# Attention and expert layer on one core: the first loads split over two DMA queues, with fewer products of ones

## Chip, cores, metric

The kernel runs on one core of a Trainium2 chip. The metric is the device time of one execution in microseconds (us); lower is better. "Rows" of a DMA are the contiguous pieces that it moves, one or more for each of the 128 partitions.

## What is computed

Two layers on 4096 tokens (2 batches of 2048) of width 512, all in float32: cross attention with relu in place of softmax against 128 context rows for each batch, and a mixture of eight experts of which each token uses two.

```python
h  = layernorm(x)
qp = relu(h @ Wq + bq); kp = relu(ctx @ Wk + bk); vp = relu(ctx @ Wv + bv)
s  = relu(qp @ kp.T) / sqrt(512) + mask
x  = x + relu(s @ vp)
h  = layernorm(x)
topv, topi = top_k(h @ gate_w, 2);  w = softmax(topv)
x  = x + sum over the two chosen experts e of  w_e * ((silu(h @ Wu[e]) * (h @ Wv[e])) @ Wo[e])
```

## The kernel before, in words

Everything is written out by hand, engine by engine, with semaphores: each engine (TensorE `pe`, ScalarE `act`, VectorE `dve`, GpSimd `pool`, and the sync engine `sp`, which issues DMAs) runs its own list in order. The order of work is thus the order of the calls in each list.

The attention part goes over the tokens in 16 blocks of 256 (`body(Step(n))` on each engine): normalise x (`norm1`), turn it (`turn_x`), project it to queries (`queries`), form scores against the keys, attend. The products of blocks are made as three products of halves of the numbers (a high part HI, written by ScalarE's `copy`, and the rest LO, written by VectorE's `sub`). Then 71 tiles of 128 tokens, sorted by expert, go through the expert layer (`tile_body`). GpSimd scatters rows of the second norm to DRAM and stores the results with indirect DMAs.

Before the first block stands a prologue, and the change lies in it:

- **sp** (lines 440 to 449) issues the loads: the context `ctxT` (128 partitions, rows of 1 KB, 512 KB in all), the key weights `wk_raw` in four quarters of 256 KB (rows of 2 KB), block 0 of x into `xin` (512 KB, rows of 2 KB), the key bias `bk_sb`, the value weights `wv_raw` (1 MB), the query weights `wq_raw` in two halves of 512 KB, and the value bias. Then follow small constants, block 1 of x (line 469), the mask and the first expert's weights.
- **pe** (lines 1755 to 1763) first multiplies a tile of ones by itself (line 1757, result unused), then runs `keys()` (16 products of 128x256 for four chunks c of the context's width, line 1557), `values(0)` (4 products of 128x512, line 1565), `turn_x` of block 0 (line 1543), `values(1)`, and the first block's `queries` (lines 1547 to 1549).
- **act** runs `norm1(Step(0), 1)` (line 802: normalises one of the two tiles of x of block 0), then `relu_key` for the four key banks (line 788), then the high parts of the query weights (line 782, tile `wq`), of the turned x (`qT`), of the keys (`kpT`), and of the values.
- **dve** waits for block 0 of x, takes its statistics (`moments1`, lines 1158 to 1166), waits for GpSimd's reciprocal root (line 662), writes `nmr` (line 1170) and the other tile of the normalised x (line 1311), then the low parts of the query weights, the value sum of batch 0 (line 1000, tile `zb`), the low parts of `qT` and `kpT` (all line 979), the value sum of batch 1, and goes on to the statistics of block 1.

On ScalarE the norm of block 0 stands ahead of `relu_key` in the list:

```python
            norm1(Step(0), 1)
            act.wait_ge(w_loaded["bk"], 16)
            for m in (2, 3, 0, 1):
                relu_key(m)
            for c in range(DC):
                act.wait_ge(w_loaded[f"wq{c // 2}"], 16)
                copy(wq[:, HI, c, :], wq_raw[:, c, :], wq_hi)
```

Of the kernel before, what the change touches and what calls it, by code (L numbers as in the profile page):

```python
# [14 lines left out]
P = 128  # L15
LOG_P = 7
D = 512
DC = D // P
# [60 lines left out]
def ge(eng, sem, value):  # L79

    if value <= 0:
        return
    eng.wait_ge(sem, value)
# [22 lines left out]
def moe_block(nc, x, ctx_in, mask, kq, kk, kv, bq, bk, bv, gate_w, Wu, Wv, Wo, out):  # L106
    ctx = ExitStack()
    with ctx:
# [6 lines left out]
        def sem(name):  # L115
            return ctx.enter_context(nc.semaphore(name))
# [38 lines left out]
        zT, ctxT = zT_ctxT[:, 0, :, :], zT_ctxT[:, 1, :, :]  # L155
# [8 lines left out]
        def raw(e):  # L164

            return wuv[:, e, :, :].rearrange("p h n -> p (h n)").bitcast(F32)

        wk_raw = raw(E - 1).rearrange("p (c n) -> p c n", c=DC)
        wv_raw = raw(E - 2).rearrange("p (c n) -> p c n", c=DC)
# [109 lines left out]
        conv_ready = sem("conv_ready")  # L279
        ones_ready = sem("ones_ready")  # L280
        ones_used = sem("ones_used")
        w_loaded = {k: sem(f"load_{k}") for k in ("ctx", "wk0", "wk1", "wk2", "wk3", "wq0", "wq1", "wv", "bk", "small", "bv")}
        wq_hi = sem("wq_hi")
        wq_ready = sem("wq_ready")
        k_done = sem("k_done")
# [89 lines left out]
        w_v = {k: w.rearrange("a b (c p) n -> p (a b c) n", p=P) for k, w in (("q", kq), ("k", kk), ("v", kv))}  # L375
# [33 lines left out]
        def x_of(b):  # L409

            return xbuf[b.x]
# [25 lines left out]

        @block.sync
        def _(sp):
            sp.dma_start(ctxT[:, :, :], ctx_in.rearrange("(c p) k -> p c k", p=P)).then_inc(w_loaded["ctx"], 16)  # L440
            for c in range(DC):
                sp.dma_start(wk_raw[:, c, :], w_v["k"][:, c, :]).then_inc(w_loaded[f"wk{c}"], 16)
            sp.dma_start(xin[:, 0, :, :], x_blk[0]).then_inc(x_loaded[0], 16)
            sp.dma_start(bk_sb[:, :], bk).then_inc(w_loaded["bk"], 16)
            sp.dma_start(wv_raw, w_v["v"]).then_inc(w_loaded["wv"], 16)
            for h in range(2):
                sp.dma_start(wq_raw[:, 2 * h:2 * h + 2, :], w_v["q"][:, 2 * h:2 * h + 2, :]).then_inc(w_loaded[f"wq{h}"], 16)
            sp.dma_start(bv_rows, bv.rearrange("(a n) -> a n", a=1).broadcast_to([P, D])).then_inc(w_loaded["bv"], 16)
# [67 lines left out]
            def load_z(t):  # L516
                for g, (first, _) in enumerate(PARTS):
                    if t == first:
                        part_ready(g)
                if t == 0:  # L520
                    sp.wait_ge(xn_turned, 2 * NB)
                if t == 2:
                    sp.wait_ge(q_done, DC * NB)
                if t == 9:
                    sp.wait_ge(s_done, NB)
                if t == 15:
                    sp.wait_ge(o_done, 2 * NB)
                if t == 18:
                    sp.wait_ge(stage_lo, 3 * E)
                q = t % RING  # L530
                if t >= RING:
                    sp.wait_ge(res_stored[q], landed(t - RING))
                    if is_held(t - RING):
                        sp.wait_ge(aside_stored, 16 * (t - RING - FULL + 1))
                sp.dma_start(zg_of(t), z_dram[bass.ds(row_of(t), P)]).then_inc(z_loaded[q], 16)
# [244 lines left out]
        def _(act):  # L780
# [18 lines left out]
            def norm1(b, t):  # L799

                ge(act, nmr1_ready, b.n + 1)
                nc.scalar.activation(xn[:, t, 0:D], x_of(b)[:, t, :], ACT.Identity, bias=nmr1[:, t:t + 1],
                                     scale=rstd1[:, t:t + 1]).then_inc((xn0_ready, xn1_ready)[t], 1)
# [30 lines left out]
            def expert_high(b):  # L834
                if b.p == 0:
                    act.wait_ge(stageA_loaded, 32 * (b.j + 1))
                else:
                    act.wait_ge(stageB_loaded, 48 * (b.j + 1))
                for dst, src in expert_parts(b):
                    copy(dst(HI), src, stage_hi)  # L840
# [27 lines left out]
            def body(b):  # L868
# [47 lines left out]
                if nxt.real:  # L916
                    expert_high(nxt)

            norm1(Step(0), 1)
            act.wait_ge(w_loaded["bk"], 16)  # L920
            for m in (2, 3, 0, 1):
# [619 lines left out]
        def _(pe):  # L1541
# [8 lines left out]

            def keys():

                pe.wait_ge(w_loaded["ctx"], 16)
                for c in range(DC):
                    pe.wait_ge(w_loaded[f"wk{c}"], 16)
                    for m in range(DC):
                        ins = pe.matmul(ps_key[m][:, 0:BT], wk_raw[:, c, m * P:(m + 1) * P], ctxT[:, c, :],
                                        start=(c == 0), stop=(c == DC - 1))
                ins.then_inc(k_done, 1)

            def values(g):

                pe.wait_ge(w_loaded["wv"], 16)
                for c in range(DC):
                    ins = pe.matmul(ps_out[g][:, :], ctxT[:, c, g * KEYS:(g + 1) * KEYS], wv_raw[:, c, :],
                                    start=(c == 0), stop=(c == DC - 1))
                ins.then_inc(v_done, 1)
# [141 lines left out]
            def expert_of(t):  # L1709
                if t not in expert:  # L1710
                    for g, (first, _) in enumerate(PARTS):
                        if t == first:
                            pe.wait_ge(sched_ready, 2 * (g + 1))
                    expert[t] = pe.value_load(sched_exp[0:1, t:t + 1], min_val=0, max_val=E - 1)
                return expert[t]
# [37 lines left out]
                    expert_of(0)  # L1753

            pe.wait_ge(ones_ready, 1)
            for n in (D, D, P):
                ins = pe.matmul(psT[0][:, 0:n], xn[:, 0, 0:P], xn[:, 0, 0:n], start=True, stop=True)
            ins.then_inc(ones_used, 1)
            keys()
            values(0)  # L1760
            pe.wait_ge(const_ready, CONSTS)
            turn_x(Step(0))
            values(1)
            for n in range(NB):
                body(Step(n))
# [63 lines left out]
```

## Time and profile before

| | |
|---|---|
| time, median of 3 runs | 416.95 us (416.0 to 418.0) |
| time of the profiled execution | 416.64 us |
| its span in the profile | 414.9 us |
| TensorE busy | 398.1 us (96%) |
| VectorE / ScalarE / GpSimd busy | 331.6 / 277.8 / 210.3 us |
| moved by DMA | 87.66 MB, mean 211 GB/s |

Times in the profile count from the start of the span. A busy share is an average over stages with different limits; the chain of waits, which is followed back from the last instruction, says what set the time in a given stretch. Ends of matmuls are modelled, so the starts are the safer numbers. In float32 one matmul of the program stands as two records in the profile. "Landing" is the moment at which a DMA's semaphore is complete.

### The profile page before, as it was taken

The page shows a single profiled execution, that of the slowest core. Times are in us where ns is not written, and L with a number is a line of the kernel's source. Part 1 is how long each engine was busy: PE and PEld are TensorE (multiplying, and loading weights), DVE is VectorE, ACT ScalarE, POOL GpSimd, SP SyncE. Part 2 cuts the span into 40 slices and gives each one's busy share as a digit, 9 for nine tenths or more (in the row PEclk, how much of TensorE's full clock was granted, in tenths as well). Part 3 has the DMA queues.
Part 4 walks back from the last instruction along what each step waited for, and adds up shares of the span by engine and source line. Part 5 has one row for each costly group of instructions (what it writes and reads, how often), then busy time and mean ns, then how long its engine had stood idle before and what let it go on. Part 6 is the DMA issues. An engine that isn't in the chain of part 4 may idle for free.

```text
span 414.9 us, 10266 instructions
## 1 busy us (share of the span) xinstructions
PE 398.1 (96%) x3031; PEld 356.1 (86%) x3031; DVE 331.6 (80%) x1108; ACT 277.8 (67%) x596; POOL 210.3 (51%) x227
## 2 busy tenths in 40 slices
PE   8999999999999999999999999999999999999980
PEld 5588899999999999998878988898999999999960
DVE  2678899999999999998787888877887666666760
ACT  1777888888998888888767666666676444444420
POOL 3011125666555565655435545453333567778882
PEclk9999999999999999999999999999999999999995
DMA  7813424677666766443695359779976799997794
GB/s 286 284 65 102 137 92 167 243 256 245 247 233 228 256 212 225 172 164 136 186 315 204 132 187 372 293 267 315 306 237 183 209 242 291 287 248 118 109 108 90
DMA packets 49557, 87.66 MB, mean 211 GB/s; under 512 B 7648, under 2 KB 18400, under 8 KB 49376
## 3 DMA queue, kind: packets, MB, share of 16 engines
q1 hardware_dynamic: 35600, 52.37, 38.9%
q0 software_dynamic: 13904, 34.62, 29.4%
q8 instruction: 28, 0.46, 0.5%
q14 instruction: 25, 0.20, 0.1%
HBM read 44.77 MB, written 48.29 MB: 224 GB/s over the span
## 4 chain that ended last, share of the span: by engine, by line
PE 69%; DVE 15%; issue 5%; ACT 4%; POOL 4%; POOLq 0%; DVEq 0%; ACTq 0%
PE psQ L1547 12%; PE psQ L1548 11%; PE psQ L1549 11%; PE psT L1543 11%; DVE qT L979 2%; PE psO L1547 2%; DVE st L1158 2%; POOL out_dram L686 2%; PE psO L1548 2%; PE psO L1549 2%; PE psZ L1547 2%; PE psZ L1549 2%; PE psZ L1548 2%; PE psQ L1543 2%; PE psS L1547 2%
## 5 line engine op out<-in xcount | busy, mean ns | idle before, releaser
L979 DVE TENSOR_TENSOR qT<-psT,qT 128x512 fp32r<-128x512 f32 x103 | 69.5, 689 | 27.2 <-ACT qT L782 26.8
L629 POOL DMA_INDIRECT z_dram<-zb x64 | 69.3, 1083 | 39.1 <-DVE zb L1267 21.4
L1547 PE MATMUL psQ<-wuv,qT 128*128 x284 | 86.3, 304 | 0.8 <-DVE qT L979 0.4
L1548 PE MATMUL psQ<-wuv,qT 128*128 x284 | 80.2, 283 | 0.0
L1549 PE MATMUL psQ<-wuv,qT 128*128 x284 | 80.1, 282 | 0.0
L1547 PE MATMUL psQ<-qT,wq 128*128 128x256 f32 x256 | 75.2, 294 | 1.5 <-DVE qT L979 1.4
L1549 PE MATMUL psQ<-qT,wq 128*128 128x256 f32 x256 | 72.4, 283 | 0.0
L1548 PE MATMUL psQ<-qT,wq 128*128 128x256 f32 x256 | 72.3, 283 | 0.0
L782 ACT ACTIVATE qT<-psT 128x512 fp32r<-128x512 f32 x103 | 59.4, 593 | 12.1 <-PE psT L1543 12.1
L1547 PEld LDWEIGHTS psQ<-wuv,qT 128*128 128x128 f32 x284 | 53.7, 189 | 5.5 <-issue 1.4
L850 ACT ACTIVATE gate_work<-psQ 128x128 f32<-128x128 f32 x71 | 19.7, 277 | 54.5 <-PE psQ L1549 54.4
L1548 PEld LDWEIGHTS psQ<-wuv,qT 128*128 128x128 f32 x284 | 54.0, 190 | 0.0
L1549 PEld LDWEIGHTS psQ<-wuv,qT 128*128 128x128 f32 x284 | 54.0, 190 | 0.0
L1547 PEld LDWEIGHTS psQ<-qT,wq 128*128 128x128 f32 x256 | 48.9, 191 | 2.4 <-DVE qT L979 2.1
L1548 PEld LDWEIGHTS psQ<-qT,wq 128*128 128x128 f32 x256 | 49.0, 191 | 0.3 <-issue 0.2
L1549 PEld LDWEIGHTS psQ<-qT,wq 128*128 128x128 f32 x256 | 48.9, 191 | 0.0
L686 POOL DMA_INDIRECT out_dram<-wq_flat x24 | 31.3, 1303 | 19.3 <-issue 8.0
L662 POOL TENSOR_TENSOR rstd<-ve,minus_half 128x2 f32<-128x2 f32 x16 | 13.2, 824 | 42.1 <-DVE ve L1166 41.2
L657 POOL TENSOR_TENSOR rstd<-ve,minus_half 128x2 f32<-128x2 f32 x16 | 12.5, 781 | 43.2 <-DVE ve L1166 43.2
L1279 DVE TENSOR_TENSOR gate_work<-gate_work,psQ 128x128 f32<-128x128 f32 x71 | 20.4, 287 | 17.5 <-ACT gate_work L850 16.7
L782 ACT ACTIVATE lgT<-psQ 128x128 fp32r<-128x128 f32 x71 | 19.7, 278 | 19.3 <-PE psQ L1543 18.8
L875 ACT ACTIVATE key_rows<-psQ,bq_sb 128x256 f32<-128x256 f32 x64 | 29.8, 466 | 2.4 <-PE psQ L1549 1.9
(305 smaller groups left out, 1064.6 us busy)
## 6 DMA issues: line engine op xcount, KB each, us to landing
wq_flat<-z_dram SPq DMA_DIRECT2D x28, 264.0 KB, 4.2
xin<-in_x_dram SPq DMA_DIRECT2D x11, 512.0 KB, 3.6
z_dram<-spare SPq DMA_DIRECT2D x17, 264.0 KB, 4.0
qpT_flat<-z_dram SPq DMA_DIRECT2D x11, 264.0 KB, 3.5
zT_ctxT<-in_x_dram SPq DMA_DIRECT2D x5, 512.0 KB, 3.7
kpT_flat<-z_dram SPq DMA_DIRECT2D x9, 264.0 KB, 3.5
vp_flat<-z_dram SPq DMA_DIRECT2D x9, 264.0 KB, 4.1
xn<-z_dram SPq DMA_DIRECT2D x8, 264.0 KB, 4.5
```

The source lines that it names most:

```text
L629: pool.indirect_dma_start(out=z_dram, out_offset=bass.IndirectOffsetOnAxis(ap=z_of(b)[:, t, ROW_COL + k:ROW_COL + k + 1].bitcast(U32), axi ...
L662: nc.gpsimd.tensor_tensor(rstd1[:, :], ve1[:, :], minus_half[:, :], ALU.pow).then_inc(rstd1_ready, 1)
L686: pool.indirect_dma_start(out=out_rows, out_offset=bass.IndirectOffsetOnAxis(ap=zg_of(t)[:, TOK_COL:TOK_COL + 1].bitcast(U32), axis=0), in ...
L782: nc.scalar.activation(o, i, ACT.Copy).then_inc(s, 1)
L850: nc.scalar.activation(sil[:, t % 2, :], psQ[t % 2][:, 0:R], ACT.Silu).then_inc(silu_done, 1)
L875: nc.scalar.activation(tq[:, m % 2, :], psQ[m % 2][:, 0:BT], ACT.Relu, bias=bq_sb[:, m:m + 1]).then_inc(qp_relu, 1)
L979: nc.vector.tensor_tensor(o, a, b, ALU.subtract).then_inc(s, 1)
L1279: nc.vector.tensor_tensor(s_tok[:, t % 2, :], sil[:, t % 2, :], psQ[t % 2][:, R:2 * R], ALU.mult).then_inc(s_ready, 1)
L1543: return pe.transpose(o, i, ident[0:n, 0:n])
L1547: pe.matmul(o, w[LO], a[HI], start=first, stop=False)
L1548: pe.matmul(o, w[HI], a[LO], start=False, stop=False)
L1549: return pe.matmul(o, w[HI], a[HI], start=False, stop=last)
```

## The change

The sync engine loads the context in four quarters instead of as a whole, and no longer loads key and value weights. ScalarE issues those at the start of its list: key weights in four quarters, value weights in two halves. TensorE waits for the context and the value weights piece by piece. The products with ones are two (512 and 256 columns) instead of three (512, 512 and 128).

```diff
         @block.sync
         def _(sp):
-            sp.dma_start(ctxT[:, :, :], ctx_in.rearrange("(c p) k -> p c k", p=P)).then_inc(w_loaded["ctx"], 16)
+            ctx_v = ctx_in.rearrange("(c p) k -> p c k", p=P)
             for c in range(DC):
-                sp.dma_start(wk_raw[:, c, :], w_v["k"][:, c, :]).then_inc(w_loaded[f"wk{c}"], 16)
+                sp.dma_start(ctxT[:, c, :], ctx_v[:, c, :]).then_inc(w_loaded[f"ctx{c}"], 16)
             sp.dma_start(xin[:, 0, :, :], x_blk[0]).then_inc(x_loaded[0], 16)
             sp.dma_start(bk_sb[:, :], bk).then_inc(w_loaded["bk"], 16)
-            sp.dma_start(wv_raw, w_v["v"]).then_inc(w_loaded["wv"], 16)
@@ block.scalar
+            for c in range(DC):
+                act.dma_start(wk_raw[:, c, :], w_v["k"][:, c, :]).then_inc(w_loaded[f"wk{c}"], 16)
+            for h in range(2):
+                act.dma_start(wv_raw[:, 2 * h:2 * h + 2, :], w_v["v"][:, 2 * h:2 * h + 2, :]).then_inc(w_loaded[f"wv{h}"], 16)
             norm1(Step(0), 1)
             act.wait_ge(w_loaded["bk"], 16)
@@ block.tensor
             def keys():
-                pe.wait_ge(w_loaded["ctx"], 16)
                 for c in range(DC):
+                    pe.wait_ge(w_loaded[f"ctx{c}"], 16)
                     pe.wait_ge(w_loaded[f"wk{c}"], 16)
@@
             def values(g):
-                pe.wait_ge(w_loaded["wv"], 16)
                 for c in range(DC):
+                    pe.wait_ge(w_loaded[f"wv{c // 2}"], 16)
@@
             pe.wait_ge(ones_ready, 1)
-            for n in (D, D, P):
+            for n in (D, D // 2):
                 ins = pe.matmul(psT[0][:, 0:n], xn[:, 0, 0:P], xn[:, 0, 0:n], start=True, stop=True)
```

ScalarE's list at the start of the changed kernel, with what each row waits for (`wuv` is the buffer that holds the raw weights, `load_` names the semaphores of the loads):

```order
L919 DMA wuv<-in_L_xattn_kernel_k_dram 128x512 x4
L921 DMA wuv<-in_L_xattn_kernel_v_dram 128x2x512 x2
L801 ACT_TABLE_LOAD
L801 ACTIVATE xn<-xin,nmr,rstd 128x512 [waits nmr1_ready]
L787 ACTIVATE key_rows<-psQ,bk_sb 128x256 [waits k_done,load_bk]
L787 ACTIVATE key_rows<-psQ,bk_sb 128x256 [waits k_done]
L787 ACTIVATE key_rows<-psS,bk_sb 128x256 [waits k_done]
L787 ACTIVATE key_rows<-psG,bk_sb 128x256 [waits k_done]
L781 ACTIVATE wq<-wuv 128x512 [waits load_wq0] x2
```

Before, the list began with the table load; the six DMAs ahead of it are new, and the rows behind it stand in the same order.

The sync engine's list at the start, before:

```order
L440 DMA zT_ctxT<-in_ctx_dram 128x4x256
L442 DMA wuv<-in_L_xattn_kernel_k_dram 128x512 x4
L443 DMA xin<-in_x_dram 128x2x512
L444 DMA bk_sb<-in_L_xattn_bias_k_dram 128x4
L445 DMA wuv<-in_L_xattn_kernel_v_dram 128x4x512
L447 DMA wuv<-in_L_xattn_kernel_q_dram 128x2x512 x2
L448 DMA wuv<-in_L_xattn_bias_v_dram 128x512
```

and of the changed kernel:

```order
L442 DMA zT_ctxT<-in_ctx_dram 128x256 x4
L443 DMA xin<-in_x_dram 128x2x512
L444 DMA bk_sb<-in_L_xattn_bias_k_dram 128x4
L446 DMA wuv<-in_L_xattn_kernel_q_dram 128x2x512 x2
L447 DMA wuv<-in_L_xattn_bias_v_dram 128x512
```

In this queue x of block 0 now follows the context directly, and the query weights follow x; the key and value weights are in the other queue.

## Rows read from the trace of the kernel before

**Rows 1.** The page: span, chain that ended last by engine.
```profile
span 414.9 us, 10266 instructions
...
PE 69%; DVE 15%; issue 5%; ACT 4%; POOL 4%; POOLq 0%; DVEq 0%; ACTq 0%
```
**Rows 2.** Chain that ended last, 0 to 60 us: start, length, what.
```profile
1.52 4.21 PE psT L1757 x6
5.73 0.68 PE psS L1557 x2
...
12.99 1.56 ACT key_rows L788 x4
14.55 0.53 ACT wq L782
...
15.10 1.59 DVE wq L979 x3
...
20.73 0.69 DVE zb L1000
...
43.25 0.44 DVE lgT L979
43.73 0.50 PE psO L1547
```
**Rows 3.** Timeline of ACT, 0 to 20 us: start, length, instruction, idle before and releaser.
```profile
0.80 1.28 ACT L802 ACT_TABLE_LOAD   x1 [0.80 <-PEq L1816]
11.93 0.81 ACT L802 ACTIVATE xn<-xin,nmr,rstd 128x512 f32<-128x512 f32 x1 [9.84 <-DVE nmr L1170]
12.99 0.84 ACT L788 ACTIVATE key_rows<-psQ,bk_sb 128x256 f32<-128x256 f32 x2 [0.25 <-PE psQ L1557]
```
**Rows 4.** Timeline of DVE, 8 to 21 us.
```profile
8.98 0.69 DVE L1158 BATCH_NORM_STATS2 st<-xin 128x6 f32<-128x512 f32 x1 [4.49 <-DMA xin<-in_x_dram]
...
18.72 0.68 DVE L979 TENSOR_TENSOR qT<-psT,qT 128x512 fp32r<-128x512 f32 x1
```
**Rows 5.** Timeline of SP's queue, 0 to 25 us: issue, time on the queue.
```profile
0.81 0.46 SPq L440 DMA_DIRECT2D zT_ctxT<-in_ctx_dram  x1
1.33 1.91 SPq L442 DMA_DIRECT2D wuv<-in_L_xattn_kernel_k_dram  x4
3.28 0.43 SPq L443 DMA_DIRECT2D xin<-in_x_dram  x1
...
4.27 0.43 SPq L445 DMA_DIRECT2D wuv<-in_L_xattn_kernel_v_dram  x1
4.75 1.02 SPq L447 DMA_DIRECT2D wuv<-in_L_xattn_kernel_q_dram  x2
```
**Rows 6.** DMA issues, 2 to 6 us: count, KB each, us from issue to landing.
```profile
wuv<-in_L_xattn_kernel_v_dram SPq DMA_DIRECT2D x1, 1024.0 KB, 7.4
wuv<-in_L_xattn_kernel_q_dram SPq DMA_DIRECT2D x2, 512.0 KB, 8.6
wuv<-in_L_xattn_kernel_k_dram SPq DMA_DIRECT2D x3, 256.0 KB, 4.4
xin<-in_x_dram SPq DMA_DIRECT2D x1, 512.0 KB, 5.6
```
**Rows 7.** The same view, 0 to 30 us: the context.
```profile
zT_ctxT<-in_ctx_dram SPq DMA_DIRECT2D x1, 512.0 KB, 3.9
```
**Rows 8.** Stretches: length, busy PE, PEld, DVE, ACT, POOL, granted clock, DMA share, GB/s.
```profile
1.52:5.53 4.01, 4.01 (x6) 1.88 (x7) 0.52 (x6) 0.56 (x1) 2.25 (x19) 1.00 0.78 280
5.53:6.25 0.72, 0.72 (x4) 0.67 (x4) 0.00 (x0) 0.00 (x0) 0.00 (x0) 1.00 1.06 393
6.25:12.72 6.47, 6.47 (x31) 5.70 (x30) 2.42 (x7) 0.80 (x1) 0.72 (x1) 1.00 1.05 381
...
4.00:14.00 10.00, 10.00 (x39) 7.64 (x38) 2.91 (x13) 1.83 (x4) 0.72 (x1) 1.00 1.05 387
```
**Rows 9.** Timeline of all engines: where values(0) and the first queries start on PE.
```profile
12.72 3.60 PE L1565 MATMUL psO<-wuv,zT_ctxT 128*128 128x512 f32 x8
...
20.06 0.68 PE L1547 MATMUL psQ<-qT,wq 128*128 128x256 f32 x1
```
**Rows 10.** DMA queues, 181.2 to 181.6 us: packets, MB, share (SP's queue: rows of 1 KB).
```profile
q0 software_dynamic: 23, 0.10, 58.9%
q1 hardware_dynamic: 47, 0.04, 36.7%
```
**Rows 11.** DMA queues, 220.0 to 220.8 us (SP's queue: rows of 2.1 KB).
```profile
DMA packets 117, 0.33 MB, mean 417 GB/s; under 512 B 17, under 2 KB 17, under 8 KB 116
...
q0 software_dynamic: 57, 0.22, 65.9%
q1 hardware_dynamic: 59, 0.10, 34.2%
```

More of the change, by code:

```diff
@@ L281, in moe_block @@
         ones_used = sem("ones_used")
-        w_loaded = {k: sem(f"load_{k}") for k in ("ctx", "wk0", "wk1", "wk2", "wk3", "wq0", "wq1", "wv", "bk", "small", "bv")}
+        w_loaded = {k: sem(f"load_{k}") for k in ("ctx0", "ctx1", "ctx2", "ctx3", "wk0", "wk1", "wk2", "wk3", "wq0", "wq1", "wv0", "wv1", "bk", "small", "bv")}
         wq_hi = sem("wq_hi")
```

## Prediction
> **What bounds the kernel now.** I read the page first: TensorE has 69% of the chain that ended last [rows 1], so the kernel as a whole is bound by products. But the change touches only the first 13 us, so the view that counts is the chain in that stretch, in order of time [rows 2]. The reader is to see a relay there: TensorE (ones from 1.52, keys from 5.53) up to 12.9 us, then ScalarE's four `relu_key` from 12.99, its copy of the query weights, VectorE's work on them from 15.10, and so on between VectorE and ScalarE until 43.73, where TensorE takes the chain over for most of the rest. There is no gap in it, so a start of `relu_key` that moves by some amount moves the end of the kernel by about that amount; what happens on TensorE ahead of 12.99 counts only as far as it moves that start.
>
> The second thing to see is in ScalarE's timeline [rows 3]. `relu_key` waited only 0.25 us for TensorE. The instruction ahead of it in ScalarE's list, the norm of block 0, ran from 11.93 to 12.74 and had waited for VectorE's `nmr`; and that goes back to VectorE's statistics, which began at 8.98 right behind the landing of x of block 0 [rows 4], issued at 3.28 and landed 5.6 us later, at 8.88 [rows 5, 6]. So two paths arrive almost together: keys at 12.90, x at 12.74. From the landing of x to the start of that norm it is 11.93 - 8.88 = 3.05 us, to its end 3.86 us.
>
> The third thing is the loads. From 4 to 14 us the DMA engines are full, with a share of 1.05 at 387 GB/s [rows 8], and all of it is one queue in its own order: context, key weights, x, value weights, query weights [rows 5]. So an order of loads can be changed here, but not their sum.
>
> **The change part by part.**
>
> *Fewer ones.* 1152 columns took from 1.52 to 5.53, 4.01 us [rows 8], or 3.48 ns a column; 768 take 2.67 us and end at 4.19, so 1.34 us of TensorE work go. The granted clock of this stretch reads 1.00 in the row, but the durations say otherwise: the keys from 6.25 to 12.72 are 30 records in 6.47 us, 0.431 us for a product (two records) of 256 columns or 1.68 ns a column [rows 8]. The ones thus ran at half the rate, at the lower of the clock's two levels. The first key product took 0.72 us, between 0.43 and the 0.89 of the lower level, so the clock rose at about 6.1 us, after some 4.6 us of unbroken products.
>
> *Keys earlier.* They need a quarter of the context and of the key weights. The whole context (0.52 MB) landed at 0.81 + 3.9 = 4.71 [rows 5, 7]; the first two quarters are 0.39 MB, 0.13 MB less, at 387 GB/s 0.34 us sooner: 4.4 us. (If the queues share bytes equally, 4.7.) Keys start at 4.4 instead of 5.53. With the clock still rising at 6.1, 1.7 us at 0.89 make 1.9 products, and the other 14.1 take 6.08 us: keys end at 12.2 instead of 12.7 (the start of values(0) [rows 9]). The later quarters are no limit: all of context and key weights, 1.57 MB, landed by about 7.3 before (the last quarter issued at 2.8, 4.4 later [rows 5, 6]), and the last quarter is wanted at about 10.4.
>
> *Six DMAs on ScalarE.* SP's issues take 0.43 to 0.49 us each [rows 5], so six cost 2.9 us there, and the table load of 1.28 us now ends at about 5.0. ScalarE sat idle 9.84 us up to 11.93 [rows 3], so this costs nothing; without that cover it would be 2.9 us. SP issues two DMAs fewer and waits for nothing.
>
> *x behind a shared queue.* This is the term that decides. Before, 2.10 MB (context, key weights, x) had to move for x to land. Now SP's queue holds context and x, ScalarE's key and value weights, and how the engines divide themselves between the two queues the trace of before cannot show, since ScalarE had none. I bound it. If both get equal bytes, x (1.05 MB into its queue) lands after the same 2.10 MB: 8.88, no change. If the engines take a row of each in turn, SP's 512 rows of 1 KB and 256 rows of 2 KB go along with 768 rows of 2 KB, 1.57 MB, so 2.62 MB must move first: 0.52 MB more at 387 GB/s, 1.35 us, landing at 10.23. The nearest rows are stretches in which SP's queue and GpSimd's are both at work: with rows of 1 KB SP's moved 0.04 MB against 0.10 [rows 10], with rows of 2.1 KB 0.10 against 0.22 [rows 11]. Bytes are not equal in either, and the queue with the smaller packets falls behind; so I take the row by row end. At that end the norm starts at 13.28 and ends at 14.09, and `relu_key` starts at 14.09 instead of 12.99: **+1.1 us**. The 0.7 us by which keys come earlier then lie in ScalarE's wait and are worth nothing.
>
> On this the Trainium skill has a rule, in "DMA: Bandwidth & Descriptors", section "Queues, rings and completion order": an engine serves the queues that have work in turn, a packet from each. Equal packets for both would give the sum above, equal bytes the rival below; the two stretches lean to the first. The same page, section "Issuing engines are not separate DMA queues", speaks against the change as a whole: loads started from several engines share the same 16 DMA engines and save only issue time. By it the 387 GB/s stay.
>
> *Value and query weights.* Row by row the first half of the value weights lands with x at 10.2, the second 1.05 MB (2.7 us) later at about 13.0, and is wanted two products into values(0), at 12.2 + 1.7 = 13.9; no wait. The query weights landed up to about 5.3 + 8.6 = 13.9 before [rows 5, 6]; the bytes up to them are the same, and they are wanted from 15.5 on. TensorE gets through values(0), turning and values(1) in the 7.34 us that it took before [rows 9], at 19.5, and then waits for the low part of `qT`, which VectorE ended at 19.40 [rows 4] and now ends at 20.5: the queries of block 0 start about 0.5 us late, and VectorE's work behind them 1.1 us late.
>
> The sum: 416.64 us of the profiled execution + 1.1 = **417.7 us**. The profiled execution is 0.3 us below the median of 416.95, and the runs lie 1.0 us to either side of that. A measurement of this kernel can tell about 0.5%, 2.1 us, from no change.
>
> **The rivals.**
>
> 1. *x lands on time* (equal bytes, or whole pieces of a DMA in turn with x ahead of the value weights). `relu_key` then starts at 12.74, when ScalarE is free, not at 12.2: 0.25 us gained, 416.4 us. For it: nothing in the trace excludes it. Against: rows 10 and 11.
>
> 2. *The two queues together move more.* In rows 11 both queues reach 417 GB/s, against 387. Row by row, 2.62 MB at 417 take 6.28 us, against 5.42 for 2.10 MB at 387: x 0.86 us late, +0.6, 417.2 us. If x also keeps its turn, it lands before 8.88 and the keys at 12.2 become the limit: 0.7 us gained, 415.9 us.
>
> 3. *Slower: TensorE's clock stays at its lower level through the keys.* The place is `keys()`. Before, it rose after unbroken products; now there are 0.2 us of nothing between ones and keys at 4.2, and more if the first quarters land late. All 16 products at 0.89 us are 14.2 us, keys end at 18.6 and `relu_key` starts at 18.9, 5.9 us late: 422.5 us. If the clock rises at T, the keys end at 0.516 T + 9.0; from T = 9.3 on they and not x hold up `relu_key`, and from 11.2 on the kernel is over 0.5% slower. Against it: the keys follow almost at once.
>
> **How the numbers follow.** Row by row, +0.6 to +1.35: 0.55. x on time: 0.30. More from both queues together, x early: 0.08. Clock low: 0.07, of which 0.05 over the bound. All but the last lie within 0.5%, where the spread of runs adds 0.03 on the fast side and 0.04 on the slow: faster 0.03, same 0.88, slower 0.09. The range reaches from the second rival, 415.9, less 0.3 for the spread, to row by row at its upper end, 416.64 + 1.35 = 418.0, and 1.0 for the spread: 415.6 to 419.0.
>
> **What would show it.** Right: VectorE's statistics of x start near 10.3 instead of 8.98; ScalarE's norm at 13.3 has waited for `nmr`, and `relu_key` follows it at 14.1 with no wait for TensorE; the keys start at 4.4 and end at 12.2; TensorE waits about 1 us for `qT` ahead of its first queries; the DMA rate from 4 to 14 us stays near 387. Wrong: statistics at 9.0 or before (first rival), a rate well above 400 (second), key products of 0.89 us beyond 6.1 (third). A change of more than 2 us with `relu_key` near 13 to 14 would mean that the chain does not carry the start to the end.

## Result and profile after

Over 22 runs of each kernel the changed one has a median of 419.16 us (417.43 to 421.33), the one before 417.52 us (416.00 to 419.14); the ratio is 1.0033, with a 95% interval of 1.0017 to 1.005. It is slower by 0.33%, about 1.4 us (0.7 to 2.1 by the interval; the two medians alone lie 1.64 us apart), where 1.1 us slower was forecast: within the 0.5% that a single measurement can tell from no change, and clear of zero only because the runs are many. The absolute median lies 0.16 above the end of the range, but the kernel before ran 0.57 us higher here than in the three runs on which the range stood; the ratio on 416.95 gives 418.3. The profiled execution took 417.43 us, the shortest of the 22, with a span of 415.7 against 414.9 us [rows 1].

ScalarE at the start of the changed kernel (timeline: start, length, instruction, idle before and releaser) answers to [rows 3]:

```profile
0.80 1.88 ACTq L919 DMA_DIRECT2D wuv<-in_L_xattn_kernel_k_dram  x4
2.70 0.98 ACTq L921 DMA_DIRECT2D wuv<-in_L_xattn_kernel_v_dram  x2
3.71 1.28 ACT L801 ACT_TABLE_LOAD   x1 [3.71 <-issue]
13.25 0.81 ACT L801 ACTIVATE xn<-xin,nmr,rstd 128x512 f32<-128x512 f32 x1 [8.25 <-DVE nmr L1173]
13.97 0.82 ACT L787 ACTIVATE key_rows<-psQ,bk_sb 128x256 f32<-128x256 f32 x2
```

The norm of block 0 starts at 13.25 instead of 11.93, and `relu_key` follows it at 13.97 with no wait for TensorE, where it had waited 0.25 us. The chain that ended last (start, length, what) now begins with the load of x, not with TensorE [rows 2]:

```profile
2.67 7.54 DMA xin<-in_x_dram
10.31 0.70 DVE st L1161
...
13.97 1.55 ACT key_rows L787 x4
...
44.59 0.50 PE psO L1550
```

x lands at 2.67 + 7.54 = 10.21, and TensorE takes the chain over at 44.59 instead of 43.73 [rows 2], 0.86 us late. From here on I use this start of the first attend (`psO`, TensorE's first product of scores and values) as the measure of the prologue in every profile: it carries what the prologue does, and leaves out what executions do differently further on.

TensorE's timeline answers to [rows 9] and to the keys in [rows 2]:

```profile
1.52 2.93 PE L1760 MATMUL psT<-xn 128*128 128x512 f32 x4 [1.52 <-DVE xn L984]
4.24 1.06 PE L1560 MATMUL psS<-zT_ctxT,wuv 128*128 128x256 f32 x2
...
5.94 1.87 PE L1560 MATMUL psQ<-zT_ctxT,wuv 128*128 128x256 f32 x4
7.65 0.59 PE L1560 MATMUL psS<-zT_ctxT,wuv 128*128 128x256 f32 x2
...
12.83 3.60 PE L1568 MATMUL psO<-wuv,zT_ctxT 128*128 128x512 f32 x8
...
20.41 0.44 PE L1550 MATMUL psQ<-qT,wq 128*128 128x256 f32 x1
```

The keys start 1.29 us earlier, at 4.24, and end no earlier: values(0) starts at 12.83 against 12.72. The whole first quarter of the keys ran at the lower level of the clock, up to about 7.6 us: from 4.24 to 5.94 and from 5.94 to 7.65 it takes 0.85 us for a product, later 0.43. (The granted clock reads 1.00 in the rows of this stretch too; the starts of the products tell.)

The loads by stretches (length, busy time of five engines, granted clock, DMA share, GB/s) answer to the last line of [rows 8]; the first line here is the lowest microsecond of the kernel before between 3 and 10 us, the others are of the changed kernel:

```profile
6.00:7.00 1.00, 1.00 (x6) 0.87 (x6) 0.00 (x0) 0.00 (x0) 0.00 (x0) 1.00 1.03 367
...
5.00:6.00 1.00, 1.00 (x4) 0.73 (x4) 0.00 (x0) 0.00 (x0) 0.00 (x0) 1.00 0.81 244
...
4.00:14.00 10.00, 10.00 (x37) 8.05 (x36) 2.90 (x13) 1.75 (x3) 0.72 (x1) 1.00 1.03 366
```

The rate is not 387 but 366 GB/s, with a hole: 244 GB/s between 5 and 6 us. The prediction had not reckoned with that. (Where an expectation below says "a second", it means a stretch of one microsecond.)

### The profile page after: what moved, and what is told of

It reads as the page before. It is cut to its first block, busy times and chain, and to the rows that moved or that the text cites. A ratio compares the mean times of both kernels' runs of the same rounds, so it can differ in the third digit from the quotient of the medians.

```text
span 415.7 us, 10269 instructions
## 1 busy us (share of the span) xinstructions
PE 398.0 (96%) x3029; PEld 356.6 (86%) x3029; DVE 330.9 (80%) x1108; ACT 277.4 (67%) x596; POOL 210.4 (51%) x227
## 4 chain that ended last, share of the span: by engine, by line
PE 64%; DVE 16%; issue 6%; ACT 4%; POOL 4%; DMA 3%; SPq 1%; POOLq 0%; DVEq 0%
PE psQ L1550 11%; PE psQ L1551 11%; PE psQ L1552 11%; PE psT L1546 10%; DVE st L1161 3%; DVE qT L982 3%; POOL out_dram L685 2%; PE psO L1550 2%; PE psO L1551 2%; PE psO L1552 2%; PE psZ L1550 2%; PE psZ L1551 2%; PE psZ L1552 2%; DMA xin<-in_x_dram 2%; PE psQ L1546 2%
```

## Experiments

Ratios are to the kernel before, with 95% intervals. The theory was: x shares the DMA engines with the value weights, lands late, and the chain carries that to the end.

**Values back on the sync engine.**

```diff
+            for h in range(2):
+                sp.dma_start(wv_raw[:, 2 * h:2 * h + 2, :], w_v["v"][:, 2 * h:2 * h + 2, :]).then_inc(w_loaded[f"wv{h}"], 16)
@@ block.scalar
-            for h in range(2):
-                act.dma_start(wv_raw[:, 2 * h:2 * h + 2, :], w_v["v"][:, 2 * h:2 * h + 2, :]).then_inc(w_loaded[f"wv{h}"], 16)
```

> The changed kernel with the two value weight loads back on the sync engine, behind x and the key bias; context by quarters there, key weights by quarters on ScalarE and two products of ones stay. Theory (x shares the engines with the value weights, lands 1.3 us late, and relu_key starts when x is normed): x now has only context and key weights beside it, 2.10 MB in all, and lands at 8.9 to 9.2 us; relu_key starts at 12.8 to 13.1, bound by keys and norm together; time within 0.1% of before (ratio 0.999 to 1.001). Rival (the shorter row of ones and the clock that rises later cost the time): x lands early as well, but the ratio stays near 1.003.

Ratio 1.0007 (0.9984 to 1.003). Timelines of VectorE and ScalarE, and the chain:

```profile
9.23 0.69 DVE L1161 BATCH_NORM_STATS2 st<-xin 128x6 f32<-128x512 f32 x1 [4.74 <-DMA xin<-in_x_dram]
...
12.17 0.81 ACT L803 ACTIVATE xn<-xin,nmr,rstd 128x512 f32<-128x512 f32 x1 [8.21 <-DVE nmr L1173]
12.89 0.82 ACT L789 ACTIVATE key_rows<-psQ,bk_sb 128x256 f32<-128x256 f32 x2
...
43.52 0.50 PE psO L1550
```

With x out of the way of the value weights, `relu_key` is back at 12.89 and the attend at 43.52, 0.2 us ahead of before; ones, keys and the second queue for key weights are as in the changed kernel. So in this profile the loss goes with the value weights' place, not with the ones. The interval alone would not exclude the changed kernel's lower bound; the place in the chain does the telling, and that is one execution. The hole was shallow in it (302 GB/s at the lowest).

**Three products of ones.**

```diff
-            for n in (D, D // 2):
+            for n in (D, D, P):
```

> The changed kernel with the three products of ones of before; its loads are kept. Theory (x decides): keys start at 5.5 instead of 4.2 and end at 12.7 to 13.0, which nobody on the chain waits for; relu_key still starts near 14.0; ratio to before as for the change, 1.002 to 1.005. Rival (ones and clock decide): ratio falls back to 1.000.

Ratio 1.0054 (1.0025 to 1.0083): not back to 1.000, so the ones do not make the loss. But x landed at 11.6 instead of 10.2, with the same loads, and the attend started at 45.99. VectorE's timeline:

```profile
11.69 0.70 DVE L1161 BATCH_NORM_STATS2 st<-xin 128x6 f32<-128x512 f32 x1 [7.20 <-DMA xin<-in_x_dram]
```

**The changed kernel once more**, to see whether that is chance; no edit.

> The changed kernel itself, for a second profile. In its first profile x landed at 10.2, but with the same loads and three products of ones it landed at 11.6, and the runs of the changed kernel spread over 4 us. Theory A: the landing of x varies from execution to execution because the dip in the rate does; this profile shows it between 10.0 and 12, and start of relu_key and span follow it one for one (415.7 us at 10.2). Rival: the landing is 10.2 again and the spread of times comes from later in the kernel. Ratio to before 1.002 to 1.005.

Ratio 1.0054 (1.0029 to 1.008). x landed at 11.6 again:

```profile
11.69 0.69 DVE L1161 BATCH_NORM_STATS2 st<-xin 128x6 f32<-128x512 f32 x1 [7.21 <-DMA xin<-in_x_dram]
```

```profile
15.36 1.55 ACT key_rows L787 x4
...
46.00 0.50 PE psO L1550
```

The theory of the chain holds: x is 1.38 us later than in the first profile, `relu_key` 1.39, the attend 1.41. The span is 418.8, 3.1 us longer, so the other 1.7 us come from later in the kernel: VectorE's last instruction on the results starts at 405.81 against 404.82, and GpSimd's last store at 410.69 against 407.59. The kernel is the same in both profiles, so this part is spread between executions; what makes it was not looked into. The landings of 10.2 and 11.6 give attends 0.86 and 2.27 us late; the measured 1.4 us lie between them.

**One queue, twice the delay.** The kernel before, value weights ahead of x.

```diff
+            sp.dma_start(wv_raw, w_v["v"]).then_inc(w_loaded["wv"], 16)
             sp.dma_start(xin[:, 0, :, :], x_blk[0]).then_inc(x_loaded[0], 16)
             sp.dma_start(bk_sb[:, :], bk).then_inc(w_loaded["bk"], 16)
-            sp.dma_start(wv_raw, w_v["v"]).then_inc(w_loaded["wv"], 16)
```

> The kernel before, one queue, with the value weights issued ahead of x: twice the suspected delay with no second queue, no change of ones and no change of waits. Theory: 1.05 MB more at 387 GB/s go ahead of x, 2.7 us, so x lands at 11.6, relu_key starts at 15.4, 2.4 us later; time 2.4 us or 0.6% above before (ratio 1.005 to 1.007). Rival (the chain gives the delay back further on, or the cost of the change comes from the second queue itself): ratio below 1.003.

Ratio 1.0063 (1.0035 to 1.0091), 2.6 us against 2.4 expected. Statistics of x start at 11.57, `relu_key` at 15.24, and:

```profile
45.87 0.50 PE psO L1547
```

2.14 us late. The statistics are 2.59 us late and `relu_key` 2.25, so the slack is 0.34 us and not the 0.25 of its wait in [rows 3]: behind a norm it starts 0.72 us after the norm's start (12.17 and 12.89, 13.25 and 13.97 above), so before it could have started at 12.65. A late x costs its delay less this slack, with one queue as with two, and of that the chain gives back 0.1 us by the first attend.

**Key weights in rows of 1 KB.**

```diff
             for c in range(DC):
-                act.dma_start(wk_raw[:, c, :], w_v["k"][:, c, :]).then_inc(w_loaded[f"wk{c}"], 16)
+                for r in range(2):
+                    act.dma_start(wk_raw[:, c, r * BT:(r + 1) * BT], w_v["k"][:, c, r * BT:(r + 1) * BT]).then_inc(w_loaded[f"wk{c}"], 16)
@@ keys
-                    pe.wait_ge(w_loaded[f"wk{c}"], 16)
+                    pe.wait_ge(w_loaded[f"wk{c}"], 32)
```

> The changed kernel with each quarter of the key weights loaded as two halves of its columns, rows of 1 KB instead of 2 KB; same bytes, same queues. Theory (the two queues get a row each in turn, whatever its bytes): while SP moves its 512 rows of context and 256 of x, ScalarE's queue moves 768 rows of 1 KB, 0.79 MB instead of 1.57 MB, so x lands after 1.84 MB instead of 2.62, about 2.0 us sooner, at 8.2; relu_key then waits for the keys and starts at 12.9 to 13.2; ratio to before 0.999 to 1.001. The last key weights land as late as 10.2 and are wanted at 11. Rival (the queues share bytes, or x is late because a second queue starts slowly or ScalarE's table load gets in the way): x lands near 10.2 as in the changed kernel, ratio 1.003.

Ratio 1.005 (1.0027 to 1.0073): the time was a miss. x did come 1.2 us sooner (statistics at 9.12), not 2.0, and the keys then were late: ScalarE took 4.45 us to issue the eight pieces, and TensorE waited for them and for the value weights. ScalarE's timeline, and the chain that ended last, which here goes through the value weights and not through x or `relu_key`:

```profile
13.78 0.84 ACT L787 ACTIVATE key_rows<-psQ,bk_sb 128x256 f32<-128x256 f32 x2 [0.91 <-PE psQ L1561]
...
5.83 10.55 DMA wuv<-in_L_xattn_kernel_v_dram
...
45.89 0.50 PE psO L1551
```

`relu_key` is 0.79 us late and the attend 2.16: the rest is the value weights', which landed at 16.38.

So the sharing is about the number of things in the other queue and not their bytes; whether rows or whole DMAs are counted this run hardly says, for both were doubled against the bytes.

**All loads in one queue**, quarters in turn, as a test of the hole in the rate.

```diff
             for c in range(DC):
                 sp.dma_start(ctxT[:, c, :], ctx_v[:, c, :]).then_inc(w_loaded[f"ctx{c}"], 16)
+                sp.dma_start(wk_raw[:, c, :], w_v["k"][:, c, :]).then_inc(w_loaded[f"wk{c}"], 16)
             sp.dma_start(xin[:, 0, :, :], x_blk[0]).then_inc(x_loaded[0], 16)
             sp.dma_start(bk_sb[:, :], bk).then_inc(w_loaded["bk"], 16)
+            for h in range(2):
+                sp.dma_start(wv_raw[:, 2 * h:2 * h + 2, :], w_v["v"][:, 2 * h:2 * h + 2, :]).then_inc(w_loaded[f"wv{h}"], 16)
@@ block.scalar
...
```

(ScalarE's six DMAs are taken out.)

> The changed kernel with all loads on the sync engine: context and key weights by quarters in turn, then x, the key bias, the value weights by halves, the query weights; pieces, waits and two products of ones as in the changed kernel. Theory A (x is late by its share of the engines, and a second queue also lowers the rate: the four runs with two queues so far show a second of 167 to 302 GB/s within 4 to 9 us, which the two runs with one queue do not): no such dip, the rate stays above 360 from 3 to 14 us, x lands at 8.8 to 9.0, relu_key at 12.7 to 12.9, ratio to before 0.998 to 1.000. Theory B (the rate falls because the loads come in more and smaller DMAs): the dip is there with one queue too, x lands after 9.1.

That the second queue makes the hole falls. Ratio 1.0016 (0.9988 to 1.0044), statistics at 10.43, attend at 44.75, and the hole is there with one queue. Rate and chain:

```profile
7.00:8.00 1.00, 1.00 (x7) 0.87 (x6) 0.00 (x0) 0.00 (x0) 0.00 (x0) 1.00 1.04 242
...
4.58 5.75 DMA xin<-in_x_dram
...
44.75 0.50 PE psO L1549
```

Here x lands at 10.33, as late as in the first profile of the changed kernel, with nothing beside it in a second queue.

**Context by quarters alone**, in the kernel before.

```diff
-            sp.dma_start(ctxT[:, :, :], ctx_in.rearrange("(c p) k -> p c k", p=P)).then_inc(w_loaded["ctx"], 16)
+            ctx_v = ctx_in.rearrange("(c p) k -> p c k", p=P)
+            for c in range(DC):
+                sp.dma_start(ctxT[:, c, :], ctx_v[:, c, :]).then_inc(w_loaded[f"ctx{c}"], 16)
@@ keys
-                pe.wait_ge(w_loaded["ctx"], 16)
                 for c in range(DC):
+                    pe.wait_ge(w_loaded[f"ctx{c}"], 16)
```

> The kernel before, one queue, three products of ones, with the context in four quarters ahead of the key weights and nothing else changed. If the quarters alone lower the rate: a second below 303 GB/s within 3 to 10 us, x lands at 9.5 or later instead of 8.9, relu_key follows 0.6 us or more later, ratio to before 1.001 to 1.003. If not (the dip needs loads of the two kinds in turn, or two queues): x lands at 8.8 to 9.1 and the ratio is 1.000.

Ratio 1.0024 (1.0004 to 1.0043). This one edit brings the hole and a late x, with one queue and the ones of before. Statistics, rate, attend:

```profile
10.88 0.69 DVE L1160 BATCH_NORM_STATS2 st<-xin 128x6 f32<-128x512 f32 x1 [6.39 <-DMA xin<-in_x_dram]
```

```profile
7.00:8.00 1.00, 0.99 (x5) 0.90 (x6) 0.00 (x0) 0.00 (x0) 0.00 (x0) 1.00 0.86 229
```

```profile
45.19 0.50 PE psO L1549
```

TensorE waited 1.52 us between ones and keys here, and still ran the keys at the upper level of the clock from their start (0.43 us for a product); the ones, 0.25 us shorter than before, had reached that level ahead of the wait:

```profile
1.52 3.96 PE L1759 MATMUL psT<-xn 128*128 128x512 f32 x6 [1.52 <-DVE xn L983]
7.00 0.67 PE L1559 MATMUL psS<-zT_ctxT,wuv 128*128 128x256 f32 x2 [1.52 <-DMA wuv<-in_L_xattn_kernel_k_dram]
7.51 0.59 PE L1559 MATMUL psG<-zT_ctxT,wuv 128*128 128x256 f32 x2
7.94 1.03 PE L1559 MATMUL psQ<-zT_ctxT,wuv 128*128 128x256 f32 x4
```

**Context whole in the changed kernel**, the counterpart.

```diff
-            ctx_v = ctx_in.rearrange("(c p) k -> p c k", p=P)
-            for c in range(DC):
-                sp.dma_start(ctxT[:, c, :], ctx_v[:, c, :]).then_inc(w_loaded[f"ctx{c}"], 16)
+            sp.dma_start(ctxT[:, :, :], ctx_in.rearrange("(c p) k -> p c k", p=P)).then_inc(w_loaded["ctx0"], 16)
@@ keys
-                    pe.wait_ge(w_loaded[f"ctx{c}"], 16)
+                    pe.wait_ge(w_loaded["ctx0"], 16)
```

> The changed kernel with the context loaded as one DMA again; key and value weights stay on ScalarE's queue. What is read here is the landing of x and the rate of the loads; the keys will start late, since the whole context now shares the engines with all key weights (about 7 us), so the time itself says little. All seven kernels with the context in quarters show a second below 303 GB/s within 3 to 10 us, the three with it in one DMA show none. Theory A (the quarters of the context lower the rate, the second queue only shares it): the rate stays above 340 from 3 to 12 us and x lands at 9.8 to 10.3, where row by row puts it. Theory B (two queues lower the rate as well): a dip, and x past 10.5.

The lowest rate of a microsecond from 3 to 12 us is 324 GB/s, so the theory that two queues bring the hole is out. But x landed at 8.0, two us before the place that row by row gave it:

```profile
8.00:9.00 1.00, 1.00 (x4) 0.82 (x3) 0.87 (x3) 0.00 (x0) 0.00 (x0) 1.00 0.92 324
...
8.09 0.69 DVE L1159 BATCH_NORM_STATS2 st<-xin 128x6 f32<-128x512 f32 x1 [3.61 <-DMA xin<-in_x_dram]
```

The DMA queues from 3 to 4 us (packets, MB, share; q1 is SP's, q10 ScalarE's), from 4.5 to 5 us, and from the start up to 6.9 us, when x was nearly through (1.01 of the 1.05 MB of context and x):

```profile
q1 hardware_dynamic: 323, 0.33, 94.7%
q10 hardware_dynamic: 27, 0.03, 7.6%
...
q10 hardware_dynamic: 97, 0.19, 101.7%
q1 hardware_dynamic: 11, 0.01, 4.5%
...
q1 hardware_dynamic: 767, 1.01, 42.9%
q10 hardware_dynamic: 372, 0.70, 26.4%
```

From 3 to 4 us the engines work almost on the context alone while ScalarE's queue has at least three DMAs waiting; from 4.5 to 5 us they work almost on key weights alone while x waits, issued at 1.33. They do not take a row of each; they take a DMA of each. x was nearly through after two DMAs of SP's and 0.70 MB, two to three quarters, of ScalarE's, where row by row puts 1.57 MB. In the changed kernel the same count is four quarters of the context and x against four quarters of key weights and, where ScalarE's queue has the first turn, half the value weights; its queues up to 9.45 us:

```profile
q10 hardware_dynamic: 793, 1.49, 45.5%
q1 hardware_dynamic: 840, 1.04, 33.4%
```

There row by row gives 1.57 MB and a DMA of each 1.05 or 1.57, by whose turn is first; it was 1.49, and so the sum came out right. In the run with rows of 1 KB, where row by row gives 0.79 and five DMAs against five 0.66, it was 0.70 up to 7.75 us, too near to both to choose. The Trainium skill ("DMA: Bandwidth & Descriptors", "Queues, rings and completion order") says that an engine drains a whole packet of one queue, typically 9 to 17 descriptors, before it turns to the next; this run agrees if a packet is taken to be a DMA's share on one engine, which for the whole context is 32 rows (512 rows on 16 engines), more than the typical.

The kernel's time, 1.0043 (1.0019 to 1.0067), has another cause: TensorE waited 0.69 us between ones and keys, the clock stayed at its lower level up to about 11 us, and `relu_key` waited 3.51 us for the keys:

```profile
5.13 1.22 PE L1558 MATMUL psS<-zT_ctxT,wuv 128*128 128x256 f32 x2 [0.69 <-DMA zT_ctxT<-in_ctx_dram]
...
15.37 0.84 ACT L785 ACTIVATE key_rows<-psQ,bk_sb 128x256 f32<-128x256 f32 x2 [3.51 <-PE psQ L1558]
```

**Two products of ones alone**, in the kernel before.

```diff
-            for n in (D, D, P):
+            for n in (D, D // 2):
```

> The kernel before with the two shorter products of ones and nothing else. The key weights' first quarter lands at 5.4, so TensorE waits from 4.2 to 5.5 and starts the keys when it did before. If the clock still rises near 6.1, the keys end at 12.7 and the ratio is 1.000; if the wait puts the rise off, each us of it costs 0.5 us: a rise at 7.2, as in the changed kernel, ends the keys at 13.3 and costs 0.5 us (1.001); a rise past 9 costs over 1.4 us (1.0035 or more).

Ratio 1.0025 (0.9995 to 1.0055), unclear: the eleven runs on which the ratio stands spread from 415.85 to 421.37 us. The profiled one, 421.37 us, was the longest of them, and shows the worst of the three cases, a rise of the clock at about 10.9:

```profile
5.48 1.19 PE L1557 MATMUL psS<-zT_ctxT,wuv 128*128 128x256 f32 x2 [1.03 <-DMA wuv<-in_L_xattn_kernel_k_dram]
...
9.88 1.06 PE L1557 MATMUL psG<-zT_ctxT,wuv 128*128 128x256 f32 x2
10.73 1.12 PE L1557 MATMUL psQ<-zT_ctxT,wuv 128*128 128x256 f32 x4
11.69 0.59 PE L1557 MATMUL psS<-zT_ctxT,wuv 128*128 128x256 f32 x2
```

`relu_key` started at 15.41 and the attend at 46.15, 2.4 us late. The third rival is thus real, where nothing fills the time up to the keys, but not in every execution: the shortest runs, at 415.85 and 416.35 us, are as short as the shortest of the kernel before (415.93) and leave no room for 2.4 us. In the changed kernel there is no such gap: the first key product starts at 4.24, inside the 1.52 + 2.93 us of the ones, and the earlier quarters are what lets it.

**Two tries at better order.** First, one queue as above with x ahead of the last two quarters:

```diff
             for c in range(DC):
                 sp.dma_start(ctxT[:, c, :], ctx_v[:, c, :]).then_inc(w_loaded[f"ctx{c}"], 16)
                 sp.dma_start(wk_raw[:, c, :], w_v["k"][:, c, :]).then_inc(w_loaded[f"wk{c}"], 16)
+                if c == 1:
+                    sp.dma_start(xin[:, 0, :, :], x_blk[0]).then_inc(x_loaded[0], 16)
-            sp.dma_start(xin[:, 0, :, :], x_blk[0]).then_inc(x_loaded[0], 16)
```

> As the kernel with all loads on the sync engine, with x issued between the second and the third quarter of the key weights. Theory: x lands after 1.31 MB, at about 6.8, so the norm ends at 10.6 and relu_key starts when the keys end, at 12.1 to 12.3, 0.8 us earlier than before; the last two key quarters land at 7.8 and 8.8 and are wanted at 8.6 and 10.3. TensorE's own path (7.3 us from the end of the keys to the first queries) then gives 19.5 against 20.06. Ratio to before 0.998 (0.9975 to 0.999). Rival: the clock rises later than 6 us behind the shorter ones, the keys end near 12.8 as in the changed kernel, and nothing is gained (1.000).

Ratio 1.0003 (0.9981 to 1.0025): nothing gained, as the rival had it. `relu_key` waited for keys again, which ended at 13.03, with the clock rising near 7 us:

```profile
13.29 0.84 ACT L791 ACTIVATE key_rows<-psQ,bk_sb 128x256 f32<-128x256 f32 x2 [1.06 <-PE psQ L1560]
```

Second, context by halves in the kernel before, and ones that reach up to the keys:

```diff
-            sp.dma_start(ctxT[:, :, :], ctx_in.rearrange("(c p) k -> p c k", p=P)).then_inc(w_loaded["ctx"], 16)
+            ctx_v = ctx_in.rearrange("(c p) k -> p c k", p=P)
             for c in range(DC):
+                if c % 2 == 0:
+                    sp.dma_start(ctxT[:, c:c + 2, :], ctx_v[:, c:c + 2, :]).then_inc(w_loaded[f"ctx{c // 2}"], 16)
+                if c == 3:
+                    sp.dma_start(xin[:, 0, :, :], x_blk[0]).then_inc(x_loaded[0], 16)
                 sp.dma_start(wk_raw[:, c, :], w_v["k"][:, c, :]).then_inc(w_loaded[f"wk{c}"], 16)
-            sp.dma_start(xin[:, 0, :, :], x_blk[0]).then_inc(x_loaded[0], 16)
@@ keys
-                pe.wait_ge(w_loaded["ctx"], 16)
                 for c in range(DC):
+                    pe.wait_ge(w_loaded[f"ctx{c // 2}"], 16)
@@
-            for n in (D, D, P):
+            for n in (D, D // 2, P):
```

> A try at a version better than both: one queue; context by halves, each ahead of its two key quarters; x ahead of the last key quarter; products of ones of 512, 256 and 128 columns, so that no gap stands ahead of the keys. Without a dip in the rate: first key weights land at 4.7, keys start then and end at 12.2 to 12.4 if the clock rises at 6 to 6.5; x lands at 8.1 and its norm ends at 12.0; relu_key starts at 12.3 to 12.5 instead of 12.99, and the first attend of TensorE at 43.1 to 43.3 instead of 43.73; ratio 0.998 to 1.000. If the dip comes with halves too, or the clock rises past 7: no gain, 1.000 to 1.002.

Ratio 1.0019 (0.9995 to 1.0044). The clock rose early (from 5.61 on the keys took 0.43 us a product) and the keys went well until the last quarter; but the hole came with halves too, and x landed at 9.9:

```profile
9.98 0.69 DVE L1161 BATCH_NORM_STATS2 st<-xin 128x6 f32<-128x512 f32 x1 [5.50 <-DMA xin<-in_x_dram]
```

The attend started at 44.46. No version here beats the kernel before.

## Why the prediction held, and where not

- *The relay.* Right: the start of `relu_key` moved the first attend, and the time followed in the plainest case (one queue, twice the delay: attend 2.14 us late, time 2.6 us longer by the ratio). In ten of the eleven other profiles the two moved alike within 0.11 us, from an attend 0.2 us early to one 2.4 us late; in the eleventh, with rows of 1 KB, the value weights set the attend instead.
- *Fewer ones, keys earlier.* Ones ended and keys began as reckoned (4.24 for 4.4). "With the clock still rising at 6.1" failed: it rose at about 7.6 and 7.4 in the two profiles of the changed kernel, and the keys ended at 12.83 and 12.73 instead of 12.2; the prediction's own 0.516 T + 9.0 gives 12.9 and 12.8 for these rises. It cost nothing, since x held `relu_key` until 13.97.
- *Six DMAs on ScalarE.* Right: 2.88 us, table load through at 4.99, first work at 13.25.
- *x behind a shared queue.* The term on which the forecast stood. The sum (2.62 MB ahead, landing at 10.23, norm at 13.28, `relu_key` at 14.09) met the first profile at 10.21, 13.25 and 13.97. The step under it, "the engines take a row of each in turn", is wrong: they take a DMA of each in turn, and the context whole shows the difference. That the numbers agreed is luck, twice: five DMAs of SP's queue stood against five of ScalarE's, with the same rows; and the loads started earlier (0.62 against 0.50 MB moved from 2 to 4 us), which made up for half of what the hole took (2.08 against 2.32 MB from 4 to 10 us). The nearest rows, GpSimd's queue, could not have told turns by DMA, but with 47 packets against 23 [rows 10] they were no row of each either. That `relu_key` came 0.1 us before the forecast 14.09 goes back to the slack: it starts 0.72 us after the norm's start, not 0.81.
- *"The 387 GB/s stay."* Failed. The rate fell to 366, and in the second profile x landed at 11.6. The forecast had no such case, and landings between 10.2 and 11.6 make more than its 1.1 us.
- *How much is the shared queue's and how much the hole's* the runs do not settle. With the context in quarters and nothing in a second queue, x landed at 10.78 and 10.33 and the attend was 1.46 and 1.02 us late (ratios 1.0024 and 1.0016), so the shared queue is not needed for a late x. With quarters, and key weights alone beside x, it landed at 9.13 and nothing was lost (1.0007). With the context whole, the shared queue brought x early, at 8.0. The intervals of these ratios overlap.
- *Queries.* 0.5 us late were forecast; they start at 20.41 instead of 20.06 [rows 9], 0.35 us late.
- *Rivals.* x on time: not seen in the changed kernel. Whole pieces of a DMA in turn, its second condition, came true, but x was not ahead of the value weights: 1.49 MB of ScalarE's queue went before it, 0.44 more than all key weights. More from both queues: the rate fell. Clock low through the keys: not in the changed kernel, but the ones alone showed its price.

What stays open is why the context in pieces lowers the rate of the loads behind it. It is settled that it does: nine profiles with quarters or halves each have a microsecond of 167 to 302 GB/s within 3 to 10 us, four with the context in one DMA none below 324. What the engines wait for in that microsecond was not found. Open with it is how the loss divides, as said above.

## What to carry to other kernels

When a queue is full, its order is a schedule: a load that moves to another queue is no longer behind the others but beside them, and takes turns with what was meant to come first. Ask of each engine's list which instruction stands ahead of the one on the critical path; here the slack of a norm, 0.34 us, was worth more thought than 1.3 us of products. Products that only keep TensorE at work are too many only if the data is there when they end.

## Unexpected of the hardware

- Two queues of loads got turns by whole DMAs: with the context whole, 0.33 MB of it went through from 3 to 4 us against 0.03 MB of the other queue, and from 4.5 to 5 us 0.01 MB against 0.19.
- The same 512 KB of context in four DMAs of 128 KB instead of one lowered the rate of later loads to 229 to 309 GB/s between 4 and 8 us, with one queue (before: 367 to 419).
- In the two profiles in which TensorE waited 0.69 and 1.03 us between two products of ones and the keys, the clock stayed at its lower level until about 11 us; at 0.85 us for a product instead of 0.43 that made the first attend 2.4 us late in both. With no wait there it rose between about 5.7 (all loads in one queue) and 7.6 us (changed kernel). A wait of 1.52 us behind three products of ones, which had already brought the clock to its upper level, left it there. It is one profile each, so how much of this is chance is not shown.
